# A graph layer's adjacency kept with its ten source tiles side by side for each destination

## The reference

```python
xn = _layernorm(x, axis=-1)                                   # x: 1250 x 1024
x = x + _L0_gnn_ref(xn, src, dst, ...) + _L0_mix_ref(xn[None], ...)[0]
x = x + _L0_ffn_ref(_layernorm(x, axis=-1)[None], ...)[0]

def _gcn_conv(x, W, b, src, dst, dinv):                       # used twice in _L0_gnn_ref
    xw = x @ W
    norm = (dinv[src] * dinv[dst])[:, None]
    agg = jax.ops.segment_sum(xw[src] * norm, dst, num_segments=x.shape[0])
    agg = agg + xw * (dinv * dinv)[:, None]
    return agg + b
```

## Time and profile before

| | us |
|---|---|
| median of 2 runs | 1845.66 (1844.75 to 1846.58) |
| profiled execution | 1846.52 |
| its span in the profile | 1844.4 |
| TensorE busy (PE) | 1671.0 |
| VectorE busy (DVE) | 826.1 |
| ScalarE busy (ACT) | 525.5 |

### The profile page before, as it was taken

How to read it: one execution, slowest core, us unless ns; L and a number is a source line. 1 busy time by engine, 2 the same in 40 slices (tenths; PEclk the granted TensorE clock), 3 DMA queues, 4 the chain that set the end, 5 groups by cost and what they waited for, 6 DMA issues and landing times.

```text
span 1844.4 us, 22619 instructions
## 1 busy us (share of the span) xinstructions
PE 1671.0 (91%) x8536; PEld 1467.2 (80%) x8536; DVE 826.1 (45%) x1700; ACT 525.5 (28%) x586; POOL 87.8 (5%) x81
## 2 busy tenths in 40 slices
PE   5899899899999989999999999999899657999996
PEld 2333389899998979889898898988789646889985
DVE  7888846223441031342533425334433545444521
ACT  5421022133211131333324223242210123344441
POOL 0000000000000000000000000000000001242231
PEclk9999999999999999999999999999899866999998
DMA  2114132132205210010101101012453455676664
GB/s 95 57 61 121 60 99 69 35 104 90 76 22 143 107 68 34 16 48 24 51 21 42 51 23 44 20 51 76 170 171 96 128 182 147 186 200 185 189 159 82
DMA packets 62055, 166.33 MB, mean 90 GB/s; under 512 B 7558, under 2 KB 28394, under 8 KB 60748
## 3 DMA queue, kind: packets, MB, share of 16 engines
q1 hardware_dynamic: 53772, 137.51, 22.8%
q0 software_dynamic: 8192, 27.53, 7.0%
HBM read 116.64 MB, written 51.81 MB: 91 GB/s over the span
## 4 chain that ended last, share of the span: by engine, by line
PE 78%; DVE 10%; ACT 5%; issue 4%; DVEq 2%; DMA 1%; POOL 0%; SPq 0%; POOLq 0%; ACTq 0%
PE slot L1305 36%; PE slot L1359 10%; PE slot L1530 6%; PE slot L1540 5%; PE slot L1444 3%; PE kvb L1412 3%; PE slot L1334 3%; PE slot L1399 3%; PE kvb L1530 2%; DVE oh_src L902 2%; DVE oh_key L901 2%; PE slot L1435 2%; PE slot L1513 1%; PE lsb L1506 1%; PE slot L1391 1%
## 5 line engine op out<-in xcount | busy, mean ns | idle before, releaser
L1305 PE MATMUL slot<-big_hi,slab_h 128*128 128x418 f32 x1152 | 289.1, 359 | 26.0 <-issue 8.8
L1305 PE MATMUL slot<-big_lo,slab_h 128*128 128x418 f32 x1152 | 285.7, 356 | 0.0
L1305 PE MATMUL slot<-big_hi,slab_l 128*128 128x418 f32 x1152 | 283.4, 354 | 0.0
L1305 PEld LDWEIGHTS slot<-big_hi,slab_h 128*128 128x128 f32 x1152 | 217.3, 191 | 36.3 <-issue 9.4
L1305 PEld LDWEIGHTS slot<-big_lo,slab_h 128*128 128x128 f32 x1152 | 219.3, 190 | 3.3
L1305 PEld LDWEIGHTS slot<-big_hi,slab_l 128*128 128x128 f32 x1152 | 219.0, 190 | 3.5
L1334 PE MATMUL slot<-oh_key,oh_src 125*125 125x500 bf16 x416 | 171.2, 435 | 9.1 <-DVE oh_key L901 6.7
L1334 PEld LDWEIGHTS slot<-oh_key,oh_src 125*125 125x125 bf16 x416 | 56.5, 136 | 123.2 <-DVE oh_key L901 122.7
L901 DVE TENSOR_SCALAR oh_key<-key_iota,key 125x500 bf16<-125x500 int16 x416 | 144.0, 346 | 0.4 <-issue 0.2
L1359 PE MATMUL slot<-adj,xs_h 125*128 125x418 f32 x480 | 119.5, 357 | 4.8 <-DVE xs_l L898 4.1
L1359 PE MATMUL slot<-adj,xs_l 125*128 125x418 f32 x480 | 118.7, 356 | 0.0
(11 more groups left out here) (246 smaller groups left out, 2477.1 us busy)
## 6 DMA issues: line engine op xcount, KB each, us to landing
slab_raw<-slabs_dram SPq DMA_DIRECT2D x48, 512.0 KB, 3.6
ws_raw<-w_dram SPq DMA_DIRECT2D x36, 512.0 KB, 5.6
w_raw<-w_dram SPq DMA_DIRECT2D x9, 1024.0 KB, 4.9
gnn_d<-htmp SPq DMA_DIRECT2D x8, 627.0 KB, 3.0
gnn_in<-gnn_d SPq DMA_DIRECT2D x8, 627.0 KB, 3.9
xt<-x_dram SPq DMA_DIRECT2D x10, 448.0 KB
xn_d<-xn SPq DMA_DIRECT2D x10, 448.0 KB
xs_raw<-xn_d SPq DMA_DIRECT2D x8, 560.0 KB
```

Of the source, the lines that this page charges most:

```text
L1305: mm = ten.matmul(ps[:, 512 * q:512 * q + CW], w[a][:, kt, :], big[b][:, kt, CW * q:CW * q + CW], start=(kt == 0 and c == 0), stop=(kt == ...
```

## The change

The adjacency is stored destination by destination: for each of the 1254 destinations the ten words of the ten source tiles lie side by side. The constant `keys` is listed in the same order, so a PSUM slot of the one-hot stage holds, for each of 50 destinations, ten source tiles, and ScalarE copies it in one run. The aggregation reads 418 destinations of one source tile, now words 40 bytes apart; the degree products load their weights from words 40 bytes apart; and the two products with `shifts` read ten words 250 bytes apart for each destination.

```diff
-        adj = at("adj", R, [T, NT, NP], F32R)
+        adj = at("adj", R, [T, NP, NT], F32R)
...
-            pool.memset(adj[:, :, N:NP].bitcast(F32), 0.0).then_inc(memset_done, 1)
+            pool.memset(adj[:, N:NP, :].bitcast(F32), 0.0).then_inc(memset_done, 1)
...
-                    copy(adj[:, :, DW * t:DW * t + DW], ps[:T, 0:KW].rearrange("p (j d) -> p j d", d=DW)
+                    copy(adj[:, DW * t:DW * t + DW, :], ps[:T, 0:KW].rearrange("p (d j) -> p d j", j=NT)
                          ).then_inc(act_done, 1)
...
-                    loops = shifts[:, DW * t:DW * t + T * NT].rearrange("p (j c) -> p j c", c=T)[:, :, 0:DW]
+                    loops = shifts[:, DW * t:DW * t + T * NT].rearrange("p (j c) -> p c j", c=T)[:, 0:DW, :]
...
-                        mm = ten.matmul(lsb[:T, 2 * b:2 * b + 2], adj[:, j, T * b:T * b + T], ones_r[:T, :],
+                        mm = ten.matmul(lsb[:T, 2 * b:2 * b + 2], adj[:, T * b:T * b + T, j], ones_r[:T, :],
...
-                                                adj[:, NT - 1 - j, CW * q:CW * q + CW],
+                                                adj[:, CW * q:CW * q + CW, NT - 1 - j],
...
-        "keys": np.tile((np.arange(NT)[:, None] * KEY_STEP + np.arange(DW)[None]).reshape(1, -1), (T, 1)
+        "keys": np.tile((np.arange(NT)[None] * KEY_STEP + np.arange(DW)[:, None]).reshape(1, -1), (T, 1)
```

## The result

| | before | after |
|---|---|---|
| median of 2 runs, us | 1845.66 | 2103.78 (2103.29 to 2104.26) |
| ratio, 95% interval | 1 | 1.1398 (1.1349 to 1.1447) |
| span in the profile, us | 1844.4 | 2101.1 |

The changed kernel is 14% slower. 1995 us was predicted; the stated range, 1843 to 2345 us, holds the result, the narrower range of the likeliest case, 1985 to 2015 us, does not.

The account below looks back on a forecast made before the run. TensorE was taken to bound the kernel, the aggregation's moving words setting its pace without slack; 147.5 + 0.3 + 0.2 = +148 us on 1846.5 us gave 1995 us (+8%), range 1843 to 2345 us.

Parts of the forecast that it names:

- likeliest case: Aggregation words at twice the price, with or without the fixed 17 ns, by words or clock; 1985 to 2015 us, chance 0.44.
- Part of a doubling: Rival: a new place's cost partly overlaps the column before, 0.21 to 0.33 us a product; 1870 to 1975 us, chance 0.09.
- Only the clock falls: Rival: aggregation products take 0.348 us because the granted clock is near 0.5; counted within twice the price, chance 0.44.
- four cycles a word: Rival of four times a dense word in aggregation: 0.696 us a product, 2330 us; chance 0.24 including beyond two and a half.
- ScalarE's copy, the padding and `keys` at nothing: The rest: ScalarE's copy into `adj` as one run, padding clearing and reordered `keys` were to add 0 us.
- no-cost rival: Rival: TensorE's moving port is indifferent to the step, aggregation products stay at 0.191 us; 1847 us, chance 0.22.
- part 1: L1359's moving words at a 40-byte step: 960 aggregation products at 0.348 us instead of 0.191, +147.5 us.
- The doubling: Aggregation's moving words: one word in each 0.833 ns, a separate place for every word halving the rate; 0.348 us a product.
- beyond two and a half: Aggregation words at four times or beyond two and a half times the dense price; chance 0.24, up to 2345 us.
- parts 2 and 3: Degree weight loads, +0.3 us, and opening and closing products of each tile, +0.2 us, otherwise hidden behind VectorE's pace.
- if that cover were gone, 50 x 0.21 = 10 us: Opening and closing products (L1330, L1336): 10 us if VectorE's buffers did not hide their extra 0.21 us each.
- a step may cost nothing: Degree weight loads (L1344): a load already takes about 1 ns a word, slower than a moving column, so possibly no cost.

Follow-up runs that it names:

- e2_zdense: Changed kernel, but the 960 aggregation products stream 418 words side by side (wrong counts); 1871.2 us, 1.0148 of the kernel before.
- e8_both: Changed kernel with L1330, L1336 and the degree weights read dense, so only the aggregation reads with a step; 2076.5 us, 1.1260 of the kernel before.
- e4_fives: Changed layout with five source tiles side by side instead of ten, moving words 20 bytes apart; 2036.2 us, 1.1044 of the kernel before.
- e9_steps3: Kernel before plus timed groups of eight products at many steps, each followed by eight dense products; 418 fp32r words at 40 bytes took 434 ns.
- e7_degrees: Changed kernel with the hundred degree weight loads reading 125 words side by side (degrees differ); 2093.4 us, 1.1349 of the kernel before.
- e3_pairs: Changed layout with two source tiles side by side instead of ten, moving words 8 bytes apart; 2015.0 us, 1.0926 of the kernel before.

## Why the prediction was off

**What held.** What bounds the kernel: all of the 232.3 us of the two aggregations came through to the end, as a stretch in which nothing else stands in the chain should let them (e2_zdense, e8_both). The lack of slack: a longer read is a longer product, word for word. That the price would be paid in time for the word and not in clock: the changed kernel's products take 0.436 us with the clock at 0.50 and at 1.00. Of the rivals, "Part of a doubling" and "Only the clock falls" are out as well; four cycles a word is what bf16 costs, not fp32r. ScalarE's copy, the padding and `keys` at nothing: 587 ns a copy in the changed trace against the 589 of the earlier trace rows. The no-cost rival is out.

**What failed: the price of a word in part 1.** "Between the ends I take the price of the products at the start of the stage", 0.348 us, came out at 0.436 us: 960 x 0.088 = 84.5 us too little, most of the 109 us between 1995 and 2104. The doubling was near the truth as a floor (0.352 to 0.372 us at 8, 20, 28, 32, 64, 96 and 128 bytes). At 20 bytes it would have given the aggregation's 357 us of e4_fives within 7%. But 40 bytes lies on a hump of which the trace of before holds nothing, and the forecast took the nearest row as if two cycles were a law. The likeliest case's own range should have run up to the point where the next case began; between 2015 us and "beyond two and a half" times nothing stood, and the result, 0.436 / 0.174 = 2.5 dense columns, fell just there. That the whole range, 1843 to 2345 us, holds it is owed to its width from rival to rival, not to a price that was known.

**What failed second: the cover of parts 2 and 3.** "Hidden but for the last L1336, +0.2 us" and "I take 0.3 us" together came out at 27.3 us instead of 0.5. With the 84.5 us above that is 111 us; the 109 us between forecast and result are less because the rest of the kernel was 2.9 us shorter in the profiled execution. Two things went wrong. The bf16 products were costed at twice their price, 0.21 us more each; they take 0.92 us, 0.71 more, since bf16 words from 16 bytes on cost four cycles (e9_steps3). And the cover, four buffers of 0.42 us, was held against one product, not against what queues up at a boundary with degrees: closing product, ten loads and opening product, 3.84 us in the changed chain against 1.50 before. Ten times VectorE ran out of buffers, 20.1 us in all. The sentence "if that cover were gone, 50 x 0.21 = 10 us" had the mechanism and too small a price. The degree loads alone are worth 10.4 us (e7_degrees), with the upper end I gave, 1.7 ns a word, about right: 1.97 us for ten of 125 words is 1.6 ns. Dense, though, a load inside the stage takes 0.8 ns a word, not the 1 ns read from the last block, so "a step may cost nothing" leaned on the one block that was not typical. The last block itself is 1.12 us longer, not 0.3; its lower granted clock has a part in that.

**Small slips in the sums.** The bounds of "Part of a doubling", 0.21 and 0.33 us a product, give 1862 and 1977 us by the prediction's own working, not 1870 and 1975, and 0.278 us gives 1927, not 1930. Nothing else hangs on them.

**Two words on a line.** The Trainium skill's rule, "Advanced Engine Details and Errata", section SBUF Cachelines, pointed the right way for the change as made. Its condition for full speed does not hold for TensorE's moving operand: at 8 bytes two words lie on each 16-byte line, which the rule has as full speed, and a product took 0.371 us instead of 0.191 (e3_pairs). For weight loads the runs agree with it: 104 ns at 8 bytes against 99 dense, 210 at 16.

## What to carry to other kernels

Keep the words that a matmul streams next to each other, in fp32r one word apart and in bf16 at most 4 bytes apart. Storing two or five source tiles side by side instead of ten is no compromise, as a step of 8 bytes costs the doubling already. If one of two readers of a layout must take the step, let it be the weight load: at 8 bytes it costs next to nothing, at 40 bytes some 0.1 us for 128 words against 0.24 us for 418 moving ones. It is not free where nothing covers it: the hundred degree loads cost 10.4 us here. When a cover of a few buffers is counted on, add up everything that grows at the same point of the queue, and compare that sum with the buffers.

## What the runs showed of the hardware that was not expected

- The price of a step in moving words does not depend on the granted clock: 0.436 us a product at 0.50 (266 to 269.5 us in the changed kernel) and at 1.00. That of a step in the PSUM writes was higher at a lower clock: 0.541 us for 500 columns at a mean of 0.79, 0.421 us at 1.00.
- It is not monotonic: 354 ns at 32 bytes, 520 at 48, 380 at 56, 354 at 64 and 128. Two words' advance of 80 bytes cost 432 to 436 ns in all four ways of splitting it that were run.
- bf16 words 16 or 40 bytes apart take 735 and 737 ns for 418, fp32r words 378 and 434 ns: the narrower type is the slower one.
- A step in the PSUM writes costs a doubling as well, 0.85 ns a column at 8 bytes (0.212 us / 250) and 0.84 at 40 bytes (0.421 us / 500), against 0.42 dense.
